# A fused four-layer kernel on one core: another order of the stages in its loop, and an order of its own for the batches that leave the loop

## The reference, cut to what matters

```python
x = x + tanh(g_xattn[0]) * L0_xattn(layernorm(x), ctx, ctx)     # relu attention, no softmax, 77 keys
x = x + tanh(g_ffn[0])   * L0_ffn(layernorm(x))                 # three layers of +1/-1 weights: 512-1024-1024-256
x = x + tanh(g_xattn[1]) * L1_xattn(layernorm(x), ctx)          # argmax memory, then 16 heads with softmax
x = x + tanh(g_ffn[1])   * L1_ffn(layernorm(x))                 # 64 experts, top 8, 128 rows each, and a shared expert
```

## Time and profile before

| what | value |
|---|---|
| time, three runs | 1707.98, 1708.49 (median), 1712.31 us |
| the profiled execution | 1710.62 us, span 1708.9 us |
| instructions | 50224 |
| PE, DVE, ACT, POOL busy | 90%, 77%, 60%, 59% of the span |
| steps in the hardware loop | 27 |

### The profile page before, as it was taken

One profiled execution on the slowest core, in us unless ns is written; L12 is line 12 of the kernel. 1 busy time (PEld: TensorE's weight loads), 2 busy tenths in 40 slices (PEclk: granted clock), 3 DMA queues, 4 the chain that ended last, 5 costly groups with the idle time before them and its releaser, 6 DMA issues.

```text
span 1708.9 us, 50224 instructions
## 1 busy us (share of the span) xinstructions
PE 1533.9 (90%) x15780; PEld 1308.4 (77%) x15780; DVE 1312.4 (77%) x4611; ACT 1018.1 (60%) x2789; POOL 1006.8 (59%) x1517
## 2 busy tenths in 40 slices
PE   2879999999999999999999999999999986478885
PEld 1768888888888888888888888888888865367774
DVE  5468888888888888888888888888888865456564
ACT  2456666666666666666666666666666653334443
POOL 3114566666666666666666666666666644365554
PEclk8989999999999999999999999999999997799998
DMA  7624444444433333433333333333333334558886
GB/s 224 190 55 101 101 102 100 93 98 99 87 74 79 84 82 83 92 77 77 80 84 80 84 77 77 77 80 81 80 81 77 91 67 111 126 139 207 201 196 129
DMA packets 382151, 176.21 MB, mean 103 GB/s; under 512 B 310175, under 2 KB 371561, under 8 KB 382104
## 3 DMA queue, kind: packets, MB, share of 16 engines
q1 hardware_dynamic: 348312, 156.45, 38.8%
q0 software_dynamic: 33792, 19.17, 6.6%
HBM read 51.63 MB, written 111.84 MB: 96 GB/s over the span
## 4 chain that ended last, share of the span: by engine, by line
PE 62%; DMA 14%; issue 8%; DVE 7%; ACT 4%; POOL 3%; SPq 1%; POOLq 0%; DVEq 0%; ACTq 0%
PE bank L1306 24%; PE bank L1200 9%; DMA out<-h_h,aid 9%; PE ps_yo L1200 7%; PE ps_yo L1322 3%; PE bank L1288 3%; DMA pt<-p_hl 3%; PE ps_m L1200 2%; PE ps_pt L1200 2%; PE ps_lg L1370 2%; PE ps_pt L1272 2%; ACT p L977 2%; POOL table L722 2%; PE ps_pt L1265 1%; PE ps_tr L1200 1%
## 5 line engine op out<-in xcount | busy, mean ns | idle before, releaser
L722 POOL DMA_INDIRECT table<-xs,slot x496 | 511.7, 1032 | 189.5 <-issue 158.3
L769 POOL TENSOR_TENSOR rs<-nt,minushalf 128x2 f32<-128x2 f32 x128 | 95.6, 747 | 311.4 <-DVE nt L1756 310.9
L977 ACT ACTIVATE p<-ps_lg,rmax 128x77 f32<-128x77 f32 x1024 | 248.6, 335 | 50.9 <-DVE rmax L1868 49.4
L1306 PE MATMUL bank<-h_h,held 128*128 128x256 f16 x2048 | 266.2, 273 | 1.4 <-DVE h_l L1798 1.1
L1306 PE MATMUL bank<-h_l,held 128*128 128x256 f16 x2048 | 265.7, 273 | 0.0
L1306 PEld LDWEIGHTS bank<-h_l,held 128*128 128x128 f16 x2048 | 200.6, 98 | 23.4
L1306 PEld LDWEIGHTS bank<-h_h,held 128*128 128x128 f16 x2048 | 195.4, 98 | 27.6 <-issue 1.6
L1798 DVE SCALAR_TENSOR_TENSOR h_l<-bank,h_h 128x512 f16<-128x512 f32 x256 | 172.7, 684 | 33.3 <-ACT h_h L954 23.8
L949 ACT ACTIVATE h_h<-bank 128x512 f16<-128x512 f32 x128 | 76.4, 597 | 156.1 <-PE bank L1288 156.1
L1200 PE MATMUL bank<-xt,gu_h 128*128 128x256 f16 x1024 | 157.1, 277 | 3.1 <-DVE ac L1964 2.9
L1288 PE MATMUL bank<-xt,held 128*128 128x256 f16 x1024 | 134.1, 282 | 22.8 <-DMA xt<-rows_hl 13.4
(11 more groups left out here) (271 smaller groups left out, 3884.8 us busy)
## 6 DMA issues: line engine op xcount, KB each, us to landing
ew<-in_e_wts SPq DMA_DIRECT2D x48, 384.0 KB, 3.9
table<-xg SPq DMA_DIRECT2D x8, 1284.0 KB, 14.8
xg<-table SPq DMA_DIRECT2D x64, 160.5 KB, 3.4
xs<-xr SPq DMA_DIRECT2D x31, 320.0 KB, 2.8
x<-in_x SPq DMA_DIRECT2D x32, 256.0 KB, 2.8
out<-x SPq DMA_DIRECT2D x32, 256.0 KB
table<-xs,slot POOLq DMA_INDIRECT x496
held<-in_e_wts SPq DMA_DIRECT2D x16, 384.0 KB, 5.0
```

Of the source, the lines that this page charges most:

```text
L722: return g.indirect_dma_start(out=table, out_offset=bass.IndirectOffsetOnAxis(ap=slots[:, t, k:k + 1], axis=0), in_=rows[:, t, :], in_offs ...
L769: g.tensor_tensor(rs[i][:, :], nt[i][:, 0, :], minushalf[:, :], ALU.pow).then_inc(ln_root[i], 1)
L977: ins = a.activation(p32[r % 2][:, h * S2:(h + 1) * S2], ps_lg[:, g_, h % HB * S2:(h % HB + 1) * S2], ACT.Exp, bias=rmax[r % 2][:, h:h + 1])
L1306: ins = mm(two(bank[j % 2])[:, m % 2, :], wb1[:, k, m * P:(m + 1) * P], hp[:, k, :], start=(i == 0 and k == 0), stop=(i == 1 and k == FK - 1))
```

## The change

All five engines get another order of the same stages; no instruction of the computation is added or taken away. In the loop, the bodies of POOL, ACT, DVE and SP are cut at another point (what stood at a body's start stands now at the end of the one before, with the batch letters shifted by one), and neighbours change places. The written-out `body(NB - 1)`, `body(NB)`, ... behind the loop are replaced by lists of stages, one by one, on each engine. The core of the diff:

```diff
@@ sync, body @@
-                if on(e):
-                    pass_rows(e)
                 if on(m) and not early(m):
                     load_x(m)
-                if on(d):
-                    turn_p(2, d)
+                if on(e):
+                    store_x4(e)
+                if on(m) and not early(m):
+                    load_ctx(m)
                 if on(n) and past(n):
                     turn(1, n)
...
                 if on(c):
                     turn_p(0, c)
+                if on(d):
+                    pass_rows(d)
+                if on(c):
                     turn_p(1, c)
+                    turn_p(2, c)
@@ gpsimd, body (its new end) @@
+                if on(m):
+                    ln_coef(1, m)
+                if on(d):
+                    scatter('a', d)
...
+                    scatter('f', d)
+                if on(n):
+                    ln_coef(2, n)
+                    stack_keys(n)
@@ tensor, body @@
-                if on(d):
-                    c_lg(2, d)
                 if on(e):
                     d_gu(0, e)
                 if on(d):
-                    c_lg(3, d)
+                    c_lg(2, d)
@@ vector, body (a piece of the new order) @@
+                if on(d):
+                    d_ac(3, d)
+                if on(m):
+                    ln_moments(1, m)
+                if on(c):
+                    c_plo(1, c)
+                    c_plo(2, c)
@@ tensor, behind the loop (a piece) @@
-            body(NB - 1)
-            body(NB)
-            body(NB + 1)
...
+            c_av(3, NB - 1)
+            d_dn(0, NB - 2)
+            across(4, NB - 1)
+            d_dn(1, NB - 2)
+            c_wc(NB - 1)
             d_route(NB - 1)
             d_gu(0, NB - 1)
+            d_cp(NB - 1)
             d_gu(1, NB - 1)
             d_gu(2, NB - 1)
-            d_cp(NB - 1)
```

More of the change, by code:

```diff
@@ L1490, in body @@
                 if on(c):
-                    b_l1(5, c)
                     b_l1(6, c)
                 if on(d):
-                    c_av(0, d)
+                    c_lg(7, d)
                 if on(e):
@@ L1497, in body @@
                 if on(d):
-                    c_lg(7, d)
+                    c_av(0, d)
                 if on(e):
@@ new lines, in _ @@
+            c_av(0, NB - 3)
+            d_dn(0, NB - 4)
+            c_lg(6, NB - 3)
+            c_lg(7, NB - 3)
+            d_dn(1, NB - 4)
+            b_l1(6, NB - 2)
+            b_l1(7, NB - 2)
+            c_av(1, NB - 3)
+            b_l2(0, NB - 2)
+            b_l2(1, NB - 2)
+            c_av(2, NB - 3)
+            b_l0(0, NB - 1)
+            b_l0(1, NB - 1)
+            c_av(3, NB - 3)
+            b_l0(2, NB - 1)
+            across(4, NB - 3)
+            b_l0(3, NB - 1)
+            across(2, NB - 2)
@@ new lines, in _ @@
+            d_gu(3, NB - 3)
+            c_lg(5, NB - 2)
+            b_l1(4, NB - 1)
+            b_l1(5, NB - 1)
+            c_lg(6, NB - 2)
+            c_lg(7, NB - 2)
+            d_dn(0, NB - 3)
+            d_dn(1, NB - 3)
+            c_av(0, NB - 2)
+            d_cp(NB - 3)
+            b_l1(6, NB - 1)
+            b_l1(7, NB - 1)
+            c_av(1, NB - 2)
+            b_l2(0, NB - 1)
+            c_av(2, NB - 2)
+            b_l2(1, NB - 1)
+            c_av(3, NB - 2)
+            across(4, NB - 2)
@@ new lines, in _ @@
+            across(2, NB - 1)
+            c_wc(NB - 2)
+            c_qp(NB - 1)
+            c_am(NB - 1)
+            c_cnt(NB - 1)
+            c_vb(NB - 1)
+            c_lg(0, NB - 1)
+            c_lg(1, NB - 1)
+            d_route(NB - 2)
+            c_lg(2, NB - 1)
+            d_gu(0, NB - 2)
+            c_lg(3, NB - 1)
+            d_gu(1, NB - 2)
+            c_lg(4, NB - 1)
+            c_lg(5, NB - 1)
+            d_gu(2, NB - 2)
+            c_av(0, NB - 1)
+            c_lg(6, NB - 1)
@@ new lines, in _ @@
+            ln_shift(2, NB - 2)
+            b_l0(1, NB - 1)
+            low(4, NB - 3, att[:, :, :])
+            b_l0(2, NB - 1)
+            low(2, NB - 2, xn[2][:, :, :])
+            b_l0(3, NB - 1)
+            c_x3(NB - 3)
+            ln_sums(3, NB - 3, x3, x3_ok)
+            ln_moments(3, NB - 3)
+            c_qp(NB - 2)
+            ln_shift(3, NB - 3)
+            c_argmax(NB - 2)
+            low(3, NB - 3, xr[:, :, 0:D])
+            b_l1(0, NB - 1)
+            c_counts(NB - 2)
@@ new lines, in _ @@
+            c_norm(3, NB - 2)
+            ln_moments(2, NB - 1)
+            ln_shift(2, NB - 1)
+            low(4, NB - 2, att[:, :, :])
+            low(2, NB - 1, xn[2][:, :, :])
+            c_x3(NB - 2)
+            ln_sums(3, NB - 2, x3, x3_ok)
+            ln_moments(3, NB - 2)
+            ln_shift(3, NB - 2)
+            c_qp(NB - 1)
+            c_argmax(NB - 1)
+            low(3, NB - 2, xr[:, :, 0:D])
+            c_counts(NB - 1)
+            c_values(NB - 1)
+            c_max(0, NB - 1)
@@ new lines, in _ @@
+            c_max(1, NB - 1)
+            d_max(NB - 2)
+            c_max(2, NB - 1)
+            c_plo(0, NB - 1)
+            c_max(3, NB - 1)
+            d_gu(0, NB - 2)
+            c_max(4, NB - 1)
+            d_gu(1, NB - 2)
+            c_max(5, NB - 1)
+            c_plo(1, NB - 1)
+            d_ac(0, NB - 2)
+            d_gu(2, NB - 2)
+            c_norm(0, NB - 1)
+            c_max(6, NB - 1)
+            c_max(7, NB - 1)
+            c_plo(2, NB - 1)
+            d_choose(NB - 2)
@@ L2148, in _ @@
+            c_plo(3, NB - 1)
+            d_pos(NB - 2)
+            c_norm(1, NB - 1)
+            d_slots(NB - 2)
+            c_norm(2, NB - 1)
+            d_ac(1, NB - 2)
+            d_gu(3, NB - 2)
+            d_ac(2, NB - 2)
+            d_ac(3, NB - 2)
+            c_norm(3, NB - 1)
+            low(4, NB - 1, att[:, :, :])
+            d_x4(NB - 2)
+            c_x3(NB - 1)
+            ln_sums(3, NB - 1, x3, x3_ok)
             ln_moments(3, NB - 1)
```

579 lines of the change are left out of this document (409 added, 170 removed).

## The result

The changed kernel takes 1743.02 us (median of four, 1737.87 to 1747.45) against 1708.24 us on the same chip: ratio 1.0204, 95% interval 1.0163 to 1.0245. It is 35 us slower, where I had forecast 15 us faster. Its profiled execution took 1737.87 us, span 1735.8.

What follows compares the result with a forecast made beforehand. PE, busy 90% of the span, was taken as the bound, idling 0.67 us a loop step and 47 us in the drain. Loop 0, batch steps -12.6 and last batch -2.8, cut to -15, gave 1693.5 us; 8-in-10 range 1681 to 1707.

Steps and rivals of the forecast that it cites:

- The loop, taken at 0: Loop: instructions and durations the same, only waits can change; 0 us, with -19 us if all waits go.
- The drain, taken at -15: Behind the loop: batch steps -12.6 us and last batch -2.8, cut to -15; the experts start 15 us earlier.
- step 31: Drain, batch step 31: PE's 4.51 us wait at across(4) goes, 1 us kept for a later transpose; -3.5 us.
- step 32: Drain, batch step 32: seven loads stand behind pass_rows(29) and turn_p(2, 30); -8 us for this step and step 31 together.
- step 33: Drain, batch step 33: the 6.84 us wait for pt goes, later DVE and PE work costs 2.2; together -4.6 us.
- last batch: End of the drain: choice before d_gu(0) and places ahead of d_ac(0) and d_gu(1); about -2.8 us on slot_z.
- as foreseen (7): Sign for step 32: one PE wait of some 7 us at the last c_av for pt, behind seven loads.
- 5: Rival, loop: turn_p(1, c) late in every step, PE waits at c_av(1); 1726 us at 1.2 us a step; chance 0.10.
- 1: Rival, loop: it gains too, half of the 19 us, giving 1684 us; chance 0.12.
- 4: Rival, loop: it loses 0.4 us a step and cancels the drain, 1704 to 1708 us; chance 0.12.
- 3: Rival, drain: its wait moves, seven loads and DVE's longer list eat more than allowed; about 1702 us; chance 0.15.
- 2: Rival, loop: matmuls close up, 16% slack in PEld gives up to 185 us, 1523 us; chance 0.01.

Runs made afterwards that it cites:

- e10: Old loop on four engines, the changed kernel's order on POOL alone, and the new drain; ratio 1.0115 to the kernel before.
- e16: e12 with stack_keys(c) on POOL moved right behind ln_coef(2, c), ahead of keep_x1; ratio 1.0057 to the kernel before.
- e13: e10 with POOL's stack_keys and keep_x1 moved behind scatter g; ratio 1.0019 to the kernel before.
- e18: e12 with one edit on PE in the loop, c_cnt ahead of b_l1(2); ratio 1.0071 to the kernel before.
- e9: Old loop on four engines, the changed kernel's order on SP alone, and the new drain; ratio 1.0076 to the kernel before.
- e2: Changed kernel with c_cnt back behind b_l1(2) on PE; ratio 1.0269 to the kernel before.
- e3: Changed kernel with the path from x1 to its transpose brought forward on DVE, ACT and SP; ratio 1.0352 to the kernel before.
- e15: Changed kernel with only POOL's stack_keys and keep_x1 moved behind scatter g; ratio 1.0218 to the kernel before.
- e14: e11 with POOL's stack_keys and keep_x1 also moved behind scatter g; ratio 1.0135 to the kernel before.
- e17: e14 with turn_p(3) also ahead of store_x4 on SP, and c_cnt and c_vb in their old places on PE; ratio 1.0089 to the kernel before.
- e12: Old loop on all engines and new drain, with pass_rows(28) and turn_p(2, 29) ahead of the first four weight loads; ratio 0.9930, 1693.85 us.
- e11: Changed kernel with turn(1) ahead of store_x4 and load_ctx on SP, ln_shift(2) ahead of c_norm(3) on DVE; ratio 1.0180 to the kernel before.
- e4: Changed kernel with both the edit of e2 and that of e3; ratio 1.0399 to the kernel before.

## Why the prediction was wrong

**The loop, taken at 0: this step failed.** "Instructions and durations are the same, so only waits can change" is false twice. Durations changed: `nb` went from 0.16 us to 0.40 to 1.00 in five of nine steps of the changed kernel and to 1.11 where its neighbours on POOL alone were moved (`e10`, `e16`, and back in `e13`), and products took 1.4 to 2.5 us longer in the steps with a long wait. And I set waits to nothing without comparing what I moved with what it reads. Three things stood in the order and in the trace of before: `c_cnt` goes 1.75 us forward with 0.89 us in hand (`e18`: +0.80 us a step); on SP two issues go ahead of `turn(1)`, which followed its input by 0.06 us (`e9`: +0.5 us); x1's sums and shift go behind more DVE work, where I wrote that the transpose comes "as late as before" (1.3 us later). I checked one thing, `turn_p(1)` against `c_av(1)` with 0.3 us in hand, and it held in the quiet steps. These prices are those of one edit in the old loop; taken out of the changed kernel one at a time they give nothing back (`e2`, `e3`, `e15`), three of them together 12 us (`e14`) and all together 20 of some 47 us (`e17`; the 47 are against `e12`). So the named places are a part of the loss, and how it divides in the changed kernel stays open.

The bound "no order of the loop can give back more than 19 us, and it can lose any amount" held and should have weighed more: with 0.7 us of idle PE in a step there is hardly any room, and every edit that isn't checked is on one side. It was read from quiet steps, though; the longer ones of the 27 held another 8 us. And of the 5.0 us of waits behind it `b_l0` has 2.2, which isn't most of them. I said that I would be wrong if the step moved by over 0.3 us; it moved by 1.06.

**The drain, taken at -15: right in sum, in part by luck.** The places of batch 31 come 140.75 us behind the last `b_l1(1)` of the loop, 156.1 before: -15.4, as summed. By terms, from `across(4)` of batches 29, 30 and 31 (40.25, 88.9 and 132.2 us behind that stage before; 41.2, 84.1 and 121.2 now): step 31 was +0.9 where I had -3.5, since the transpose for `b_l0(0, 31)` behind the four loads costs 4.62 us and not 1; step 32 -5.7, where -8 for both steps leaves -4.5, and the total after two steps is -4.8; step 33 -6.2 (-4.6); last batch -4.4 (-2.8). `pass_rows` stands ahead of the loads now, and PE waits 4.72 us for the transpose behind seven loads, as foreseen (7). From the places to the first `add_out` it takes 22.5 us instead of 21.6. In the old loop the same passes give 11.6 us to the first `add_out` (`e12`: 166.2 against 177.8), so some 3 of the 14.5 us seem to be the new loop's way of handing over, for which the sum has no term.

**The rivals.** 5, the slower one with 0.10, had the side and nearly the size (1726) but another place: PE's waits for `pt` from 80 to 500 us are 7.0 us, 7.7 before, and in quiet steps held transposes for `c_av` show only in `e11` and `e14`. What is new in that stretch is x1's transpose, 13.7 us of waits and none before. 1 fell. 4 had the loop on the right side, at 0.4 us a step instead of 1.06. 3 is answered above. 2, that the products close up, fell: PE is busy 41.8 of 43.9 us in a step, near the 42.14 before, and the same 109 ns lie between products.

**The clock.** It was 0.96 from 1400 to 1440 us of the changed kernel, 0.86 from 1440 to 1480 and 0.67 from 1480 to 1520. I foresaw no change there, and can't part this from the shift of work. In the loop it fell where I had not looked, in steps with a wait of some 3 us: 0.93 instead of 1.00 and 2.5 us of products, beside the 3.28 of the wait. That agrees with the Trainium skill (TensorE: Matmul & The Clock Gate, HAM oscillation), by which idle gaps cost the clock too.

## What to carry to other kernels

When an order changes and PE has 2% of idle time, write down for every stage that moves how long its input was ready before it ran, and how far it moves; the time between ready and wanted is in the trace of before, and here it was 0.9 us or less at each place that lost. Removing the wait that the profile names can make a tuned loop slower, as it did in `e2`, `e3` and `e4`: try an edit alone in the kernel that was good, where its price is clean (`e9`, `e10`, `e16`, `e18`), not only undo it in the one that was bad. And judge loop and drain apart: a good drain hid in a kernel that was 2% slower, and with the old loop it gives the fastest version, 0.993.

## What the runs showed of the hardware

- A DVE operation of 0.16 us with both inputs in SBUF took 1.11 us while POOL ran three short operations (0.43, 0.18 and 0.60 us) back to back, and ended with the last of them. DVE operations that read PSUM beside POOL's copy kept their time (`h_l` 0.68 us with and without). The Trainium skill (SBUF — State Buffer, SBUF: two separate sides) says that VectorE with two SBUF inputs and GpSimd share a port pair by an exclusive lock, held for a whole instruction by whichever came first. The trace agrees, and shows more: `nb` could be held over three operations in a row. It wasn't always. Begun 70 to 80 ns into `kst` it took 0.40 us and ended with `kst` alone (changed kernel at 1111.99, `e16` at 1088.79), and in `e12`, begun 50 ns into the operation of 0.18 us, it lost nothing; what makes the difference wasn't tried. In the traces of all twenty kernels every `nb` over 0.3 us between 80 and 1345 us, 266 of them, ended within 0.06 us of the end of `kst` or of the copy of x.
- In the loop POOL stops for 2.9 to 5.0 us between two scatters (before: until 468.19, 771.32 and 1073.44 us), and in all twenty kernels it does so behind scatters 113, 226 and 339, whatever the order around them; behind 452, in the drain, it stops again. So the stop goes by the count of indirect DMAs and not by time or place. What POOL does then isn't in the trace. The old loop's step is 1.2 to 1.8 us longer by each, the changed one's 3.3 to 3.7; 1.4 to 1.7 us of that are products at a granted clock of 0.96 for the step, where the old loop's steps stay at 1.00.
